# A mixing stage whose rows and rounded intermediates are turned by SyncE's DMA queue, a readout with two banks, and an output stage whose last batch goes in halves

## What is computed

```python
x = x + tanh(g_xattn[0]) * L0_xattn(layernorm(x), ctx, mask)      # softmax(x ctx^T / sqrt(D), masked) @ ctx
x = x + tanh(g_ffn[0])   * L0_ffn(layernorm(x), router_w, wg, wu, wd)
x = x + tanh(g_xattn[1]) * L1_xattn(layernorm(x), ctx, Wq, bq, Wk, bk, Wv, bv, Wo, bo)   # 16 heads of 32
x = x + tanh(g_ffn[1])   * L1_ffn(layernorm(x), w1, b1, w2, b2)   # 8 experts, fixed slots, gelu
```

```python
for e in range(E):
    g, u = bitlinear(xf, wg[e]), bitlinear(xf, wu[e])
    y = bitlinear(square(relu(g)) * u, wd[e])        # the intermediate is rounded again, row by row
    out = out + where(idx == e, y, 0)
```

## Time and profile before

| What | Value |
|---|---|
| Time, median of 3 runs | 1591.31 us (1589.59 to 1591.99) |
| The profiled execution's own time | 1592.72 us |
| Its span | 1590.9 us |
| TensorE busy | 1386.6 us (87%) |
| VectorE busy | 1113.6 us (70%) |
| ScalarE busy | 918.6 us (58%) |
| GpSimd busy | 515.9 us (32%) |
| Readout stage | 249.8 to 444.7 us of the span |
| Mixing stage | 490.9 to 582.5 us |
| Output stage, from its first product | 1137.0 to 1221.4 us |

### The profile page before, as it was taken

How to read it: one execution, slowest core, us unless ns; L and a number is a source line. 1 busy time by engine, 2 the same in 40 slices (tenths; PEclk the granted TensorE clock), 3 DMA queues, 4 the chain that set the end, 5 groups by cost and what they waited for, 6 DMA issues and landing times. The chain is left out here.

```text
span 1590.9 us, 25908 instructions
## 1 busy us (share of the span) xinstructions
PE 1386.6 (87%) x9534; PEld 827.3 (52%) x9607; DVE 1113.6 (70%) x1441; ACT 918.6 (58%) x1408; POOL 515.9 (32%) x411
## 2 busy tenths in 40 slices
PE   5899896999764956889999999998785999999996
PEld 3455452444342523427767777774233666666663
DVE  6888856688755978487888787874786866556561
ACT  7787832333253854517777777777334866656450
POOL 0122210000032324138999999996500000000000
PEclk9999998999866976959999999999786999999998
DMA  6898763534275449302343444452553966766540
GB/s 232 284 293 294 239 220 78 88 73 80 40 269 192 130 127 203 119 1 61 76 100 83 91 90 84 93 151 50 169 189 140 317 201 211 238 221 196 212 141 25
DMA packets 211823, 242.71 MB, mean 153 GB/s; under 512 B 96348, under 2 KB 129247, under 8 KB 210696
## 3 DMA queue, kind: packets, MB, share of 16 engines
q1 hardware_dynamic: 205880, 215.19, 46.8%
q0 software_dynamic: 5840, 26.14, 4.8%
HBM read 169.62 MB, written 52.59 MB: 140 GB/s over the span
## 5 line engine op out<-in xcount | busy, mean ns | idle before, releaser
L1748 POOL TENSOR_TENSOR t_low<-t_e 128x1024 bf16<-128x1024 f32 x185 | 364.9, 2000 | 49.2 <-ACT t_e L1795 49.2
L1833 DVE TENSOR_REDUCE t_nmax<-t_psM 128x1 f32<-128x1024 f32 x256 | 309.7, 1222 | 75.4 <-PE t_psM L1916 73.7
L1795 ACT ACTIVATE t_e<-t_psE 128x512 f32<-128x512 f32 x512 | 277.9, 595 | 105.0 <-PE t_psE L1938 97.5
L1916 PE MATMUL t_psM<-kst,qst 96*64 96x512 bf16 x1024 | 189.7, 408 | 13.2 <-DVE t_nmax L1833 7.0
L2433 PE MATMUL e_psG<-late_flat,e_w1p 128*128 (+1 forms) x1536 | 172.8, 276 | 14.7 <-DVE e_hT L2377 10.0
L1938 PE MATMUL t_psE<-qst,kst 99*64 99x512 bf16 x1024 | 181.9, 387 | 1.4
L2433 PEld LDWEIGHTS e_psG<-late_flat,e_w1p 128*128 128x128 bf16 x1536 | 151.3, 99 | 36.6 <-DVE e_hT L2377 9.8
L1952 PE MATMUL t_psO<-t_e,vst 128*33 128x512 bf16 x768 | 163.8, 391 | 3.7 <-POOL t_low L1748 3.7
L2448 PE MATMUL e_psO<-e_w2p,e_hT 128*128 128x512 bf16 x752 | 164.9, 379 | 0.8
L1916 PEld LDWEIGHTS t_psM<-kst,qst 96*64 96x64 bf16 x1024 | 89.4, 114 | 76.9 <-DVE t_nmax L1833 35.0
L2448 PEld LDWEIGHTS e_psO<-e_w2p,e_hT 128*128 128x128 bf16 x768 | 75.1, 98 | 89.0
(11 more groups left out here) (274 smaller groups left out, 2272.5 us busy)
## 6 DMA issues: line engine op xcount, KB each, us to landing
piece<-in_L_ffn_w SPq DMA_DIRECT2D x32, 1024.0 KB, 14.2
xres<-in_L_ffn_w SPq DMA_DIRECT2D x32, 1024.0 KB, 14.8
wT<-ternary POOLq DMA_DIRECT2D x8, 1536.0 KB
kst<-keys SPq DMA_DIRECT2D x96, 128.0 KB, 3.5
c_rows<-in_ctx SPq DMA_DIRECT2D x8, 1024.0 KB, 8.5
xres<-in_L_ffn_wg SPq DMA_DIRECT2D x8, 1024.0 KB, 6.4
xres<-in_L_ffn_wu SPq DMA_DIRECT2D x8, 1024.0 KB, 6.4
xres<-in_L_ffn_wd SPq DMA_DIRECT2D x8, 1024.0 KB, 6.1
```

The source lines that it names most:

```text
L1748: nc.gpsimd.tensor_tensor(low[:, low_slot(h, u), :, :], e32[:, slot(h, u), :, :], upper(h, u), ALU.subtract).then_inc(lo_pool, 1)
L1795: nc.scalar.activation(e32[:, slot(h, u), i, :], psE[:, i, :], ACT.Exp, scale=SC).then_inc(expd, 1)
L1833: nc.vector.tensor_reduce(nmax[:, h // G % 2, h % G, u:u + 1], banks_of(place_of_max(b, m)).rearrange("p a t -> p (a t)"), AX_X, ALU.max, ...
L1916: last = nc.tensor.matmul(banks_of(place_of_max(b, m))[side * SIDE:(side + 1) * SIDE, i, :], qst[0:KR, g, h % G, s0:s0 + SIDE], kst[0:KR, ...
```

## The change

**Mixing.** The transposes of TensorE and ScalarE's copies of them are gone. SyncE issues two DMA transposes for each tile instead: `turn_x(j)` from `rows` to `xT`, and `turn_h(j)` from `hq` to `hT`, both 128x512 in 16 bits. `rows` has six slots instead of four and `xT` four instead of two. SyncE's order is four `turn_x`, `turn_h(0)`, and then for each j: `turn_x(j+4)`, `turn_h(j+1)`, `store(j)`; the 2 MB load of the query weights is moved from the front to behind `turn_h(3)`. `finish` moves from VectorE to ScalarE, which for each j does: `q_casts(j+1)`, `finish(j-1)`, `squares(j+3)`.

**Readout.** `psR` has two banks, used in turn; `read(t)` waits for `update(t-2)` instead of `update(t-1)`. No order changes.

**Output.** Batches 0 to 2 are as before, up to the transposes of batch 2. The last batch is two units of two tiles. Statistics, power, normalising and splitting are done for each unit, and TensorE's order becomes: project 12 and 13, transpose 8 and 9, project 14 and 15, transpose 10 and 11, transpose 12 to 15.

The core of the diff (what only renames loop variables, or takes the same steps one tile at a time, is left out):

```diff
-        psR = c.enter_context(nc.psum_tensor("a_psR", [P, D], F32))
+        psR = c.enter_context(nc.psum_tensor("a_psR", [P, 2, D], F32))
...
                 def read(t, par, b):
                     pe.wait_ge(p_turned[t % 2], t // 2 * 16 + 16)
-                    pe.wait_ge(updated, t + 1)
+                    pe.wait_ge(updated, t)
...
+    RB, XB = 6, 4
-        rows = sb("m_rows", [P, 4, DW], BF16)
-        xT = sb("m_xT", [P, 2, KC, P], BF16)
+        rows = sb("m_rows", [P, RB, DW], BF16)
+        xT = sb("m_xT", [P, XB, KC, P], BF16)
...
                 for j in range(NS):
-                    pool.wait_ge(xposed, j + 1)
-                    pool.wait_ge(coef_ready, j + 1)
+                    if j >= RB:
+                        pool.wait_ge(x_turned[(j - RB) % XB], (j - RB) // XB * 16 + 16)
+                        pool.wait_ge(coef_ready, j - RB + 1)
...
-                prefetch(sp)
+                def turn_x(j):
+                    sp.wait_ge(loaded[j % RB], j // RB * 16 + 16)
+                    if j >= XB:
+                        sp.wait_ge(gated, j - XB + 3)
+                    sp.dma_start_transpose(xT[:, j % XB, :, :], rows[:, j % RB, 0:D]).then_inc(x_turned[j % XB], 16)
+
+                def turn_h(j):
+                    sp.wait_ge(q_cast, j + 3)
+                    if j >= 2:
+                        sp.wait_ge(lowered, j + 1)
+                    sp.dma_start_transpose(hT[:, j % 2, :, :], hq[:, j % 2, :]).then_inc(h_turned[j % 2], 16)
+
+                for j in range(4):
+                    turn_x(j)
+                turn_h(0)
                 for j in range(NS):
+                    if j + 4 < NS:
+                        turn_x(j + 4)
+                    if j + 1 < NS:
+                        turn_h(j + 1)
+                    if j == 2:
+                        prefetch(sp)
                     store(j, j % 2)
...
+                def finish(j, par):
+                    act.wait_ge(lowered, j + 3)
+                    act.wait_ge(yscale_ready, j + 1)
+                    act.wait_ge(stored[par], j // 2 * 16 + 16)
+                    nc.scalar.activation(ys[:, par, :], psY[:, par, :], ACT.Copy, scale=yscale[:, j:j + 1]).then_inc(scaled, 1)
...
                 for j in range(NS):
-                    step(j, j % 2, NS - 1 - j)
+                    if j + 1 < NS:
+                        q_casts(j + 1, 1 - j % 2)
+                    if j >= 1:
+                        finish(j - 1, 1 - j % 2)
+                    if j + 3 < NS:
+                        squares(j + 3, 1 - j % 2)
+                finish(NS - 1, (NS - 1) % 2)
...
                 def gate_and_up(j, par):
-                    pe.wait_ge(xcopied, j + 2)
+                    pe.wait_ge(x_turned[j % XB], j // XB * 16 + 16)
                     pe.wait_ge(prod_ready, j + 1)
...
                 def down(j, par):
-                    pe.wait_ge(hcopied, j + 2)
+                    pe.wait_ge(h_turned[j % 2], j // 2 * 16 + 16)
                     pe.wait_ge(scaled, j + 1)
...
-                def step(j, par, left):
-                    h_transposes(j, par)
-                    if left >= 4:
-                        x_transposes(j + 4, j % 4)
-                    if left >= 3:
-                        gate_and_up(j + 3, 1 - par)
-                    down(j, par)
+                for j in range(NS):
+                    if j + 3 < NS:
+                        gate_and_up(j + 3, 1 - j % 2)
+                    down(j, j % 2)
...
+    units = [range(b * QD, (b + 1) * QD) for b in range(LAST)] + [range(LAST * QD, LAST * QD + 2), range(LAST * QD + 2, B * QD)]
...
+                for k in range(2):
+                    update(LAST + k)
+                    x_copy(units[LAST - 1][2 * k + 1])
+                    normalise(LAST + k)
+                    x_low(LAST + k)
+                for k in range(2):
+                    x_copy(units[LAST + k][1])
...
+                for k in range(2):
+                    for t in units[LAST + k]:
+                        project(t)
+                    for t in units[LAST - 1][2 * k:2 * k + 2]:
+                        transposes(t)
+                for k in range(2):
+                    for t in units[LAST + k]:
+                        transposes(t)
```

More of the change, by code:

```diff
@@ L1177, in _ @@
                 for j in range(NS):
-                    step(j, j % 2, NS - 1 - j, j + 4 < NS, j % 4)
+                    step(j, j % 2, NS - 1 - j, j + 4 < NS, (j + 4) % RB)
             @block.tensor
             def _(pe):
-                def x_transposes(j, slot):
-                    pe.wait_ge(loaded[slot], j // 4 * 16 + 16)
-                    pe.wait_ge(xcopied, j + 1)
-                    for k in range(KC):
-                        last = nc.tensor.transpose(psX[:, k, :], rows[:, slot, k * P:(k + 1) * P], ident[:, :])
-                    last.then_inc(xposed, 1)
                 experts = {}
@@ L2068, in _ @@
                 pool.wait_ge(half_set, 1)
-                for b in range(B):
-                    q = slice(b * QD, (b + 1) * QD)
-                    pool.wait_ge(veps_ready, b + 1)
+                for i, unit in enumerate(units):
+                    q = slice(unit.start, unit.stop)
+                    pool.wait_ge(veps_ready, i + 1)
                     nc.gpsimd.tensor_tensor(rstd[:, q], veps[:, q], half[:, q], ALU.pow).then_inc(rstd_ready, 1)
@@ L2122, in low, with update @@
                                                        cpair[:, b % 2, 0, k, :], ALU.add, ALU.subtract).then_inc(c_lo, 1)
-                def update(b):
-                    for t in range(b * QD, (b + 1) * QD):
+                def update(i):
+                    for t in units[i]:
                         dve.wait_ge(projected, t + 1)
@@ L2144, in normalise, with x_low @@
                                                 ALU.subtract, ALU.mult).then_inc(normed, 1)
-                def x_low(b):
-                    for t in range(b * QD, (b + 1) * QD):
+                def x_low(i):
+                    for t in units[i]:
                         dve.wait_ge(hi_done, t + 1)
@@ L2163, in _ @@
                 nc.vector.reciprocal(sums[:, 0, :], sums[:, 0, :]).then_inc(rsums_ready, 1)
-                for b in range(B):
+                for b in range(LAST):
                     update(b)
@@ L2189, in transposes, with project @@
[L2189 to L2198 removed]
+                def project(t):
+                    b = t // QD
+                    if t % QD == 0:
+                        pe.wait_ge(c_lo, (b + 1) * KC)
+                    if t >= 4:
+                        pe.wait_ge(updated, t - 3)
+                    n = 0
+                    for ra, rb in ((0, 0), (0, 1), (1, 0)):
+                        for k in range(KC):
+                            nc.tensor.matmul(psG[:, t % 4, :], cpair[:, b % 2, ra, k, t % QD * P:(t % QD + 1) * P],
+                                             woT[:, rb * KC + k, :], start=(n == 0), stop=False)
+                            n += 1
+                    nc.tensor.matmul(psG[:, t % 4, :], o.bones[:, :], o.brows[:, :], start=False,
+                                     stop=True).then_inc(projected, 1)
@@ new lines, in transposes @@
+                def transposes(t):
+                    pe.wait_ge(lo_done, t + 1)
+                    if t >= 2:
+                        pe.wait_ge((even_copied, odd_copied)[t % 2], t // 2)
+                    for r in range(2):
+                        for k in range(KC):
+                            last = nc.tensor.transpose(psX[:, t % 2, r * KC + k, :], xpair[:, t % 4, r, k * P:(k + 1) * P],
+                                                       ident[:, :])
+                    last.then_inc(xposed, 1)
@@ L2200, in _ @@
                 pe.wait_ge(o.bones_set, 1)
                 pe.wait_ge(o.brows_loaded, 16)
-                project(0)
-                for b in range(B):
-                    if b + 1 < B:
-                        project(b + 1)
-                    transposes(b)
+                for t in units[0]:
+                    project(t)
+                for b in range(LAST - 1):
+                    for t in units[b + 1]:
+                        project(t)
+                    for t in units[b]:
+                        transposes(t)
```

154 lines of the change are left out of this document (46 added, 108 removed).

## The result

| | Before | After |
|---|---|---|
| Time, median | 1591.65 us (1589.59 to 1592.82, 4 runs) | 1605.37 us (1603.94 to 1607.97, 4 runs) |
| Span of the profiled execution | 1590.9 us | 1603.6 us |
| Readout, first scores to the router's first product | 258.8 to 444.7 = 185.9 us | 253.7 to 435.0 = 181.3 us |
| Mixing, first gather to the issue of the last store | 491.8 to 578.7 = 86.9 us | 481.8 to 597.8 = 116.0 us |
| Output, end of splitting batch 2 to last copy done | 1198.8 to 1221.1 = 22.3 us | 1216.9 to 1232.8 = 15.9 us |

The ratio is 1.0087, with a 95% interval of 1.0073 to 1.0101. The forecast was 1590.5 us (1582 to 1600), so it was wrong: the change is slower by 0.9%, and the time lies above the range.

The account below looks back on a forecast made before the run. Mixing was taken as bound by TensorE, VectorE and ScalarE at once, readout and output by waits. Readout -5.8, output -5.4 and mixing +10.4 gave -0.8 us: 1590.5 us from a 1591.3 median, range 1582 to 1600.

Parts of the forecast that it names:

- Readout, forecast -5.8: Readout: second bank ends the 5.33 us wait; the last tile's transpose is late next; gain about 5.8 us.
- Output, forecast -5.4: Output: in halves, the last batch's update starts at 1198.8 instead of 1206.45 us; gain about 5.4 us.
- Mixing, forecast +10.4: Mixing: DMA transposes make the stage about 10.4 us longer, bounds +3.5 and +19.
- The ring: Mixing: `turn_x`, gate and up, `finish`, `store`, `turn_x` two tiles later run in a row; 3.55 us a tile instead of 3.04.
- the hole: Mixing: TensorE idle some 4.8 us where the 2 MB load, behind the third `turn_h`, holds back the transposes.
- an earlier start: Mixing start: gathers no longer share DMA with the 2 MB load; first down product 4.5 us sooner.
- The ring's clean length: Mixing: landing, gate and up, relu and square, rounding, scaling, hand-over and store sum to 7.02 us for two tiles.
- Meetings with gathers and stores add some 0.1: Mixing: transfers meeting on the same DMA engines lengthen two tiles by some 0.1 us, to 7.1.
- The first tiles, whose four `xT` are filled ahead, go at 2.6 us: -2.8 us over three tiles: Mixing start: buffers filled ahead let the first tiles go at 2.6 us each, 2.8 us less over three.
- The 2 MB load, forecast +3.0 and 1.7 for the clock: Mixing, middle: load delays transposes 3.0 us (0 to 5); TensorE at half speed after idling costs 1.7 (0 to 3.5).
- SyncE's load, forecast 2.24 us: Mixing: two transpose issues of 0.94 us and a store of 0.36 per tile, 2.24 us, below the ring's 3.55.
- rival 2: Mixing: the ring binds harder, landing 3.2 us, +8.5 us, total 1599; deciding point a landing above about 2.6; chance 0.2.

Follow-up runs that it names:

- x2: Changed kernel with only the first six row gathers, 17 of 23 left out, so the output is not the reference's: 1600.52 us, ratio 1.0056.
- x4: Changed kernel with the row transpose of tile j+5 issued on SyncE ahead of the store of tile j instead of behind it: 1594.82 us, ratio 1.0021.
- x7: Changed kernel with the 2 MB load cut into eight loads of 256 KB, behind the transposes of intermediates 3 to 10: 1603.44 us, ratio 1.0085.
- x5: Changed kernel with the scaling of the results back on VectorE, behind the quantising of two tiles later: 1603.96 us, ratio 1.0077.
- x13: Changed kernel with the edits of x4, x7 and x2 together; output is not the reference's: 1591.52 us, ratio 1.0002.
- x14: Changed kernel, only rows turned by SyncE, `turn_x(j+7)` ahead of `store(j)`, intermediates back on TensorE and ScalarE, load in eight pieces: 1573.78 us, ratio 0.9895.
- x11: Changed kernel with the old mixing stage, and the 2 MB load in eight pieces ahead of stores 1 to 8: 1576.32 us, ratio 0.9889.
- x10: Changed kernel with rows transposed on TensorE and copied by ScalarE again, intermediates still through SyncE, load in eight pieces: 1590.14 us, ratio 0.9986.
- x6: x4 with the 23 stores issued by GpSimd instead of SyncE: 1598.0 us, ratio 1.004.

## Why the prediction was wrong

**Readout, forecast -5.8.** Right: the wait, what is late next and the landing (4.3 us from 420.64 to 424.94, 4.2 taken) came as forecast; a little less was gained. It measured -4.6 in the changed kernel's trace and -5.2 on average over fifteen; the last read took 7.9 us instead of 7.2 behind the idle time.

**Output, forecast -5.4.** Right: -6.4. The power of two columns takes 0.70 us instead of the 1.0 that four columns take, and the copies fit the gaps.

**Mixing, forecast +10.4, measured +29.1.** The ring, the pacing by `store`, the hole and an earlier start were all there, and the sign of the stage was right; the size was not. Taken from down product to down product and set against the forecast's own terms, the 18.7 us between them are:

| Stretch | Forecast | Measured | Difference |
|---|---|---|---|
| First gather to first down product | 15.8 | 17.6 | +1.8 |
| The first three tiles | 7.9 | 12.6 | +4.8 |
| The tile that the load holds up | 8.3 | 11.4 | +3.2 |
| The 18 tiles behind it | 63.9 | 71.7 | +7.8 |
| Last down product to last store | 1.8 | 2.6 | +0.9 |

The remaining 0.2 to 0.3 us lie before the first gather. The terms, one by one:

1. *The ring's clean length*: 7.4 us for two tiles instead of 7.1. Landing 2.55 instead of 2.35, store to next transpose 0.41 as taken. It is 0.15 us a tile, 2.7 us of the 7.8. This term was nearly right.
2. *"Meetings with gathers and stores add some 0.1"*, for two tiles: this is the largest step that failed, the other 5.1 us of the 7.8. The gather is released by the same transpose that SyncE's next one follows, so nearly every transpose meets one: 4.52 us a tile instead of 3.70. Without gathers, in x2, the same 18 tiles take 67.1 us, 4.6 less, and the stage is 6.0 us shorter. Why a transfer beside a gather takes longer no run shows. I had priced bytes on an average and not asked which event starts the gather.
3. *"The first tiles, whose four `xT` are filled ahead, go at 2.6 us: -2.8 us over three tiles"*: this failed too, by 4.8 us. The four filled buffers serve gates 0 to 3, which all stand before the first down product, so what they gain falls there (8.5 us from gate 0 to gate 3, 9.0 before). The down products of tiles 1 to 3 follow gates 4 to 6, and the transposes for gates 5 and 6 already stand behind `store(0)` and `store(1)`: the ring binds from there, at 4.2 us a tile. In x4, whose order cuts the ring, the same three tiles take 10.8 us.
4. *The 2 MB load, forecast +3.0 and 1.7 for the clock*: gates 6 and 7 are 9.8 us apart, 6 us above the ring. In addition slow product groups came behind waits in further places (3.24 and 2.48 us at gates 10 and 16, and down groups of 1.4 to 1.9 us instead of 1.03 at tiles 7, 13 and 20 to 22); the last of them are the 0.9 us at the end. Pieces take 4.6 us off.
5. *SyncE's load, forecast 2.24 us*: I let the issue fall with size along a line through two points, 0.94 us. It is 1.22 at both sizes, and SyncE's load is 3.26 us. In the changed kernel the ring hides that, but with SyncE full the design does not reach the old step of 3.04 us; my own mark for this case, an issue above 1.3 us, was put at the wrong number because it was set for two transposes and no store.

The start gained 2.2 us at the first gate (7.1 from the first gather instead of 9.3) and 2.4 at the first down product, where 4.5 was forecast. The removals are not independent: x4 takes 14.5 us, x2 6.0, x7 4.6 and x5 3.9, but the three in x13 take 18.3 together where 25.1 is their sum, as x13's rival said of transposes that are issued earlier and so hide a late landing. Of rival 2 the mechanism was right and its deciding point too: landings are above 2.6 us for most tiles up to the last gather. Its price of 8.5 us over the forecast was half of what came, because it took one landing for all tiles and left the load's hole as it was. The range ended at 1600 by the bounds of single terms; those of mixing alone (+19) were already broken by 10 us. The chances, added up from the parts that the prediction lists, are 0.32 faster, 0.41 same and 0.27 slower, not 0.34, 0.38 and 0.28; nothing hangs on it.

The page of the Trainium skill that I had weighed, "Advanced Engine Details and Errata", section "X-Bar Transpose (TRN2)", calls transposes as fast as regular DMAs. The changed kernel shows a store and two transposes in four microseconds, 571 to 575 us in slices of 0.1 us:

```profile
GB/s 0 0 0 0 0 0 0 0 0 0 0 164 410 451 389 389 369 369 82 92 215 192 236 202 218 138 19 0 0 0 0 0 38 205 294 289 287 174 23 1
```

The store moves at 369 to 451, the row transpose right behind it at 192 to 236, and the next one, of the intermediates, which has nothing beside it, at up to 294. So the trace does not agree with the page at this size, though the forecast's 205 to 225 was not the whole truth either.

## What to carry to other kernels

Before moving work to a DMA queue, write out that queue's program and ask of each transfer what the instruction ahead of it waits for: here a store paced the next tile's input, and one line of order was worth 10 us. Transposes by DMA pay for inputs that are known several tiles ahead (x14's stage is 4.8 us shorter than x11's) and not for a value on the chain of its own tile (x10's is 12.9 us longer than x11's). Price the issue of a small transfer by the smallest size seen, not by a line through larger ones, and a meeting of transfers by the event that releases them, not by an average share.

## What was unexpected of the hardware

- One DMA transpose of 128x512 takes the queue 1.22 us, as long as one of 128x1024 (1.23), while 128x2048 took 1.82.
- The product that waits for it starts 2.5 to 2.6 us after its issue with nothing beside it, 3.5 to 5.4 us where a gather of 128 rows was under way, and 8.3 us behind two loads of 1 MB on the same queue.
- With two loads of 1 MB ahead on the queue, gates stood between 8.4 us (x5) and 13.3 us (x6) apart in every kernel that had them there; a piece of 256 KB cost the queue 0.54 us.
- The issue itself can be held up: the second transpose behind those loads took 2.70 us in the changed kernel, and the longest in x6, right behind them, 5.17 us. With the DMA share at 1.00 in x14, no product waited for a transpose.
